# Shared expert of a decoder layer moved from the third stage into the last steps of the second stage's pipeline, and the padding rows with it

## The chip, the cores and the metric

The kernel runs on one core of a Trainium2 chip. The time is the device time of one execution in microseconds (us). The core has a matrix engine (TensorE, "PE" in the profile; its weight loads are "PEld"), a vector engine (VectorE, "DVE"), an activation engine (ScalarE, "ACT"), a general engine (GpSimd, "POOL") and a queue engine (SyncE, "SP"). Each engine works through its own list of instructions in order and waits on semaphores that others raise.

## The reference, cut to what matters

16 sequences of 128 tokens, 256 features. Three sublayers follow one another, each with a residual and a layer norm:

```
x = layernorm(x + self_attention(x))            # linear and windowed attention, gated
x = layernorm(x + cross_attention(x, context))  # 16 heads of 16
x = layernorm(x + mixed(x) + shared(x))
shared(x) = (silu(x @ Wsg.T) * (x @ Wsu.T)) @ Wsd.T     # 256 -> 256 -> 256
mixed(x)  = sum over the 4 experts picked of 32: weight * down_e(silu(gate_e(x)) * up_e(x))   # 256 -> 128 -> 256
```

The router's scores are sigmoid(x @ Wr.T) plus a bias; two of four groups are kept, then four experts of them.

## The kernel before, in words

The kernel has three stages with an all-engine barrier, a clearing of semaphores and another barrier between them. Stage 1 (`decoder_kernel`) is self attention. Stage 2 (`cross_attention`) is cross attention with its layer norm, the router, and the scatter of each token's row to the four experts' row lists in DRAM (`x_rows`). Stage 3 (`expert_layer`) is the shared expert, the routed experts and the last layer norm. Every fp32 product is made of three float16 products (high x high, high x low, low x high), so that each operand is split in two, mostly the high part by ACT (a copy to float16) and the low part by DVE or POOL (a subtraction).

**Stage 2** is a software pipeline over NB = 16 tiles of 128 tokens. Each engine has a loop over steps i, whose body is a hand written order of parts, and each part works on tile i minus its lag. PE's loop has 23 steps (`range(NB + 7)`), ACT's 23, DVE's 21 (`range(NB + 5)`), and POOL's 25. A PE step i answers to DVE step i - 2 and ACT step i + 1: a tile's scores are made in PE step n + 3, its minima in DVE step n + 1 and its exponentials in ACT step n + 4. The parts that the text names: `x2_T` (transposes of the normed tile, PE), `counts` (two matmuls over the picked experts, L1614), `logits` (L1606), `out_proj` (L1590, L1508), `transposed` and `weighted` (L1564, L1576), and on DVE `chosen` (MAX8 at L1425 to the mask `selc` at L1429), `places`, `scores_`, `st`, `x2`, `payload` (up to L1467). `chosen(i - 5)` is the first part of a DVE step. POOL's `scatter` (L1191) issues four indirect DMAs a tile, after `payload`.

PSUM has eight banks. One holds the attention output, and seven are shared by turns: `ORDERS` lists for each bank the uses in the order in which they take it within a step, `LAGS` the tile that each works on, and `Turns.wait` makes PE wait until the use before has been emptied.

The last steps have less in them. Attention scores end with PE step 18, `weighted` with step 19, `out_proj` with 20, `logits` with 21, `counts` with 22.

**Stage 3** begins with four things at once. SP loads a small table (`known`), waits for `fill_row` from DVE (the first row behind each expert's last), loads 32 row numbers into registers and issues 32 DMAs that write 128 padding rows each behind the 32 experts' lists (L1738); when these have landed it issues the gathers of the routed tiles (`xg`, L1755), 20 ahead. DVE makes the table of tiles in 19 chained steps and waits for one matmul of it on PE (L1956). PE, ACT and DVE run the shared expert in NCH = 8 chunks of 256 tokens (`shared_chunk`): 24 matmuls of 256 columns for gate and up, two banks each; Silu on ACT; the product on DVE; high part on ACT; low part on DVE; 12 matmuls of 256 columns for the down product; and DVE adds the result to `xs`. PE waits for all eight additions (`pe.wait_ge(sacc_r, NCH)`) before its first routed tile. Then 96 routed tiles run in a pipeline with lags of up to 10 steps, and after them the sum, the layer norm and the output.

Of the kernel before, what the change touches and what calls it, by code (L numbers as in the profile page):

```python
# [7 lines left out]
F16 = mybir.dt.float16  # L8
# [6 lines left out]
P = 128  # L15
# [15 lines left out]
PIECES = ((0, 1, 2), (3, 4))  # L31
ROUTE_SCALE = 2.5
# [47 lines left out]
def live(n, count=NB):  # L80
    return 0 <= n < count
# [7 lines left out]
class Turns:  # L89
    def __init__(self, orders, lags, reads, emptied):  # L90
        self.orders, self.lags, self.reads, self.emptied = orders, lags, reads, emptied

    def wait(self, pe, use, n):
        i = n + self.lags[use]
        for order in self.orders:
            k = order.index(use) if use in order else 0
            while use in order and i + k // len(order) >= 0:
# [3 lines left out]
                if 0 <= tile < NB:  # L101
                    pe.wait_ge(self.emptied[prev], self.reads.get(prev, 1) * (tile + 1))
                    break


def decoder_kernel(nc, x, ctx_t, wcat, vecs, rowvecs, rel_bias, consts, masks, experts, rbias_d, out):
# [3 lines left out]
    with es:  # L110
# [846 lines left out]
        c.scattered = [sem(f"scattered{k}") for k in range(RR)]  # L957
        kept = len(stage_sems)
# [29 lines left out]
def cross_attention(nc, c, ctx_t, experts, consts, rbias_d, out):  # L988
# [4 lines left out]
    with ExitStack() as st:  # L993
        def s2(name, shape, dt=F32):
# [5 lines left out]
        x1 = s2("x1", [P, 2, 2, D], F16)  # L1000
        x1T = s2("x1T", [P, 2, 2, KT, P], F16)
# [23 lines left out]
                "XT": 0, "P0": 3, "XPK": 2, "P2": 3, "XPQ": 1}  # L1025
# [4 lines left out]
                  ["S1", "XT"],  # L1030
                  ["XT2", "XWO", "XPQ"],
                  ["S0", "XPK"]]
# [5 lines left out]
        wait_turn = Turns(ORDERS, LAGS, {"XPK": 2}, emptied).wait  # L1038
# [68 lines left out]

        with nc.Block() as block:
            @block.sync
            def _(sp):  # L1110
# [23 lines left out]
                for i in range(NB + 7):  # L1134
# [3 lines left out]
                    context(i)  # L1138

# [68 lines left out]
            def _(act):  # L1208
# [90 lines left out]
                for i in range(NB + 7):  # L1299
                    ao_high(i - 6)  # L1300
                    pT_high(i - 5, 2)
                    xv_high(i - 4)
# [16 lines left out]
                    x1T_(i - 1)  # L1319
                    xq_high(i - 2)  # L1320

            @block.vector
            def _(dve):
# [145 lines left out]
                for i in range(NB + 5):  # L1469
# [25 lines left out]
            def _(pe):  # L1495
# [121 lines left out]
                for i in range(NB + 7):  # L1617
# [13 lines left out]
                    x1_T(i)  # L1631
                    transposed(i - 3, 0)
                    k_proj(i - 2)
                    transposed(i - 3, 2)
                    q_proj(i - 1)
                    weighted(i - 3, 0)


def expert_layer(nc, c, consts, out):
# [3 lines left out]
    CT = 2  # L1643
    NCH = NB // CT
    CW = CT * P
# [8 lines left out]
    with ExitStack() as st:  # L1654
# [19 lines left out]
        fill_row = s3("fill_row", [P, NE], U32)  # L1674

        with ExitStack() as before_tail:
# [5 lines left out]
            sgate = s3t("sgate", [P, 2, KT, CW])  # L1682
# [363 lines left out]
```

## Time and profile before

| | us |
|---|---|
| median of 3 runs (801.82 to 803.7) | 803.7 |
| the profiled execution's own time | 802.68 |
| its span in the profile | 800.9 |
| stage 1 to the barrier's exit at | 270.9 |
| stage 2, up to the barrier's exit at | 557.9 |
| shared expert, up to the last addition's end at | 599.2 |
| routed tiles, up to the last matmul near | 746 |
| sum, layer norm, output, up to | 800.9 |

Positions are counted from the start of the span. The own time is 1.8 us longer than the span, for what lies around it. The mean TensorE clock granted over the run is 0.866 of full speed.

### The profile page before, as it was taken

How to read it: one execution, taken by the hardware profiler on the slowest of the kernel's cores; microseconds unless marked ns; L12 is line 12 of the kernel's file. 1: busy time of each engine (PE TensorE's matmuls, PEld its weight loads, DVE VectorE, ACT ScalarE, POOL GpSimd, SP SyncE). 2: the span in 40 equal slices, each digit the busy share in tenths (PEclk: the TensorE clock that was granted, in tenths of full speed). 3: DMA queues.
4: the chain of work that ended last, by engine and by line, in shares of the span. 5: the costliest groups of instructions: out<-in, count | busy, mean ns of one | idle time of the engine just before them, and what ended most of it. 6: DMA issues, size and time to landing. Idle time of an engine off the chain costs nothing. (4 is left out here: it accounts for less than half of the span.)

```text
span 800.9 us, 24293 instructions
## 1 busy us (share of the span) xinstructions
PE 624.3 (78%) x7778; PEld 518.9 (65%) x7778; DVE 586.5 (73%) x2170; ACT 524.8 (66%) x1542; POOL 533.2 (67%) x689
## 2 busy tenths in 40 slices
PE   3899999999998488878777888631889999999100
PEld 2688888888888366756666666421679887777100
DVE  5898888888885367999999999882546655555495
ACT  5699999898887299878787787520228765555000
POOL 5877989999898535477767766663004765556684
PEclk9899999999999789787978787655899999999655
DMA  9200000000000122333543354241942555452383
GB/s 323 64 19 2 2 3 14 21 3 3 2 2 4 46 73 68 100 114 115 147 125 119 116 155 129 93 151 55 211 135 79 148 161 154 142 170 85 139 271 117
DMA packets 57131, 77.68 MB, mean 97 GB/s; under 512 B 8488, under 2 KB 46512, under 8 KB 56880
## 3 DMA queue, kind: packets, MB, share of 16 engines
q1 hardware_dynamic: 46208, 56.37, 24.7%
q0 software_dynamic: 7680, 16.87, 5.8%
q10 hardware_dynamic: 3120, 2.88, 1.1%
q8 instruction: 67, 1.10, 0.6%
q14 instruction: 56, 0.46, 0.2%
HBM read 44.39 MB, written 27.49 MB: 90 GB/s over the span
## 5 line engine op out<-in xcount | busy, mean ns | idle before, releaser
L1772 POOL DMA_INDIRECT y_rows<-yo,xg x96 | 94.7, 986 | 98.2 <-DVE yo L1886 60.0
L1886 DVE TENSOR_SCALAR yo<-bank,xg 128x256 f32<-128x256 f32 x96 | 46.4, 484 | 57.2 <-PE bank L1995 56.7
L1259 ACT ACTIVATE scx<-bank,mnx 128x128 f32<-128x128 f32 x256 | 73.9, 408 | 18.9 <-DVE mnx L1333 18.7
L1934 PE MATMUL bank<-gT,we_hi 128*128 128x128 f16 x768 | 79.1, 219 | 4.5 <-DVE eh L1896 3.6
L500 ACT ACTIVATE sc<-sc,mn 128x128 f32<-128x128 f32 x256 | 79.6, 396 | 0.0
L1191 POOL DMA_INDIRECT x_rows<-rows,slot_ix x64 | 63.5, 992 | 21.6 <-issue 18.3
L1162 POOL TENSOR_TENSOR we_lo<-east,we_hi 128x256 f16<-128x256 f32 (+1 forms) x80 | 59.3, 768 | 11.4 <-ACT we_hi L1233 11.1
L1934 PEld LDWEIGHTS bank<-gT,we_hi 128*128 (+1 forms) x768 | 51.8, 96 | 19.9 <-issue 9.9
L674 DVE CUSTOM_DVE_ANT_0 sc<-bank,rel 128x128 f32<-128x128 f32 x256 | 57.8, 286 | 8.7 <-PE bank L783 8.6
L1808 ACT ACTIVATE gT<-bank 128x512 f16<-128x512 f16 x96 | 56.4, 591 | 7.9 <-PE bank L1985 7.7
L1813 ACT ACTIVATE eh_hi<-eh 128x128 f16<-128x128 f32 x96 | 29.7, 309 | 46.8 <-DVE eh L1896 46.2
L1564 PE MATMUL bank<-ident,scx 128*128 128x128 f32 x256 | 51.5, 340 | 2.9 <-ACT scx L1259 2.8
L1934 PE MATMUL bank<-gT,we_lo 128*128 128x128 f16 x384 | 53.1, 218 | 0.0
L1339 DVE TENSOR_TENSOR pTx_lo<-bank,pTx_hi 128x512 f16<-128x512 f32 x64 | 43.6, 681 | 5.2 <-ACT pTx_hi L1267 4.8
L683 DVE TENSOR_TENSOR pT_lo<-bank,pT_hi 128x512 f16<-128x512 f32 x64 | 43.1, 681 | 5.0 <-ACT pT_hi L507 4.9
L830 PE MATMUL bank<-hT,w_hi 128*128 128x128 f16 x384 | 42.6, 227 | 3.3 <-DVE q_lo L655 2.3
L1333 DVE TENSOR_REDUCE mnx<-bank 128x4 f32<-128x512 f32 x64 | 42.5, 673 | 1.1 <-DVE rows L1458 0.3
L507 ACT ACTIVATE pT_hi<-bank 128x512 f16<-128x512 f32 x64 | 37.9, 592 | 6.8 <-PE bank L805 5.0
L1267 ACT ACTIVATE pTx_hi<-bank 128x512 f16<-128x512 f32 x64 | 40.0, 632 | 1.9 <-PE bank L1564 1.8
L793 PE MATMUL bank<-ident,sc 128*128 128x128 f32 x256 | 40.0, 279 | 0.4 <-ACT sc L500 0.4
L1564 PEld LDWEIGHTS bank<-ident,scx 128*128 128x128 f32 x256 | 35.4, 174 | 4.6 <-ACT scx L1259 4.6
L1985 PE MATMUL bank<-ident,xg 128*128 128x128 f16 x384 | 36.6, 218 | 1.6 <-DVE xs L1876 0.8
(291 smaller groups left out, 2441.6 us busy)
## 6 DMA issues: line engine op xcount, KB each, us to landing
xg<-x_rows SPq DMA_DIRECT2D x96, 129.0 KB, 2.6
east<-in_experts SPq DMA_DIRECT2D x32, 384.0 KB, 3.5
rows<-xhl SPq DMA_DIRECT2D x16, 512.0 KB, 4.5
yg<-y_rows SPq DMA_DIRECT2D x16, 512.0 KB, 4.5
x_rows<-padrow SPq DMA_DIRECT2D x33, 129.0 KB, 4.1
wst<-in_wcat SPq DMA_DIRECT2D x8, 256.0 KB, 5.6
cst<-in_ctx_t SPq DMA_DIRECT2D x16, 128.0 KB, 3.3
out<-fin ACTq DMA_DIRECT2D x16, 128.0 KB, 3.1
```

The source lines that it names most:

```text
L500: done = act.activation(sc[:, g, j], sc[:, g, j], ACT.Exp, bias=mn[:, n % 2, g, j:j + 1], scale=-1.0)
L674: dve.tensor_tensor_reduce(out=sc[:, g, j], in0=sc_bank[g][:, j * P:(j + 1) * P], in1=rel[:, g, j], scale=-1.0, scalar=-NEG, op0=ALU.add, ...
L683: dve.tensor_tensor(pT_lo[:, g % 2], pT_bank[g][:].rearrange("p (h k) -> p h k", h=GH), pT_hi[:, g % 2], ALU.subtract).then_inc(pT_rd[g], 1)
L1162: pool.tensor_tensor(pair(shared.we_lo, piece, n), arrived(piece), pair(shared.we_hi, piece, n), ALU.subtract).then_inc(we_lo_done[k], 1)
L1191: pool.indirect_dma_start(shared.x_rows, bass.IndirectOffsetOnAxis(ap=slot_ix[:, n, k:k + 1], axis=0), rows4[:, q, k], None).then_inc(shar ...
L1259: done = act.activation(scx[:, g, j], sc_bank[g][:, j * P:(j + 1) * P], ACT.Exp, bias=mnx[:, n % 2, g, j:j + 1], scale=-1.0)
L1339: dve.tensor_tensor(pTx_lo[:, g % 2], pT_bank[g][:].rearrange("p (h k) -> p h k", h=GH), pTx_hi[:, g % 2], ALU.subtract).then_inc(xpT_rd[g ...
L1564: last = pe.transpose(pT_bank[g][:, j * P:(j + 1) * P], scx[:, g, j], ident[:])
L1772: pool.indirect_dma_start(c.y_rows, bass.IndirectOffsetOnAxis(ap=xg_word(U32, n % G, 0), axis=0), yo[:, n % YO], None, bounds_check=NDEST ...
L1808: act.activation(gT[:, n % U], GT_BANK[n % len(GT_BANK)], ACT.Copy).then_inc(gt_r, 1)
L1886: dve.tensor_scalar(yo[:, n % YO], DN_BANK[n % 2][:, 0:D], xg_word(F32, n % G, 1), None, ALU.mult).then_inc(yo_r, 1)
L1934: done = pe.matmul(o[:, m * width:(m + 1) * width], lhs(x_, k, m), rhs(y_, k, m), start=t == 0, stop=t == 5)
```

## The change

In stage 3 the shared expert and the padding rows are gone, with their buffers and semaphores. PE's first routed tile no longer waits for additions; the table's matmul is put in front of step 5 of the routed loop (`i == L_GU + 1`), in the bank of the odd down products, so the down product of tile 1 waits for the table.

In stage 2 the shared expert becomes three more uses of the shared banks: `GU0`, `GU1` (gate and up of one of the chunk's two tiles, in one bank) and `SD` (the down product). `FIRST_SH` = 17: chunk n has its gate and up products in PE step n + 17 (24 matmuls of 128 columns for each tile), its Silu in ACT step n + 18, its products and low part in DVE step n + 16, its high part in ACT step n + 19, its down product in PE step n + 18 and its addition in DVE step n + 17. The hidden tile has one buffer instead of two. The loops grow: PE to 26 steps, ACT to 27, DVE to 25. ACT's Silu and Exp now alternate: chunks 0 to 4 follow the exponentials of attention or of the router in ACT steps 18 to 22.

The row numbers of the padding are made by DVE in its step 20. SP writes half of the padding rows after its loop in stage 2, ACT the other half after its own loop. The first gathers of stage 3 wait for both.

```diff
+NCH = NB // 2
+FIRST_SH = 17
...
         LAGS = {...
-                "XT": 0, "P0": 3, "XPK": 2, "P2": 3, "XPQ": 1}
+                "XT": 0, "P0": 3, "XPK": 2, "P2": 3, "XPQ": 1, "GU0": FIRST_SH, "GU1": FIRST_SH, "SD": FIRST_SH + 1}
...
-                  ["S1", "XT"],
-                  ["XT2", "XWO", "XPQ"],
-                  ["S0", "XPK"]]
+                  ["S1", "XT", "GU0"],
+                  ["XT2", "XWO", "XPQ", "GU1"],
+                  ["S0", "XPK", "SD"]]
...
+        def pad_rows(eng, kind, part):
+            eng.wait_ge(shared.fill_r, 1)
+            _, rows = nc.values_load_multi_w_load_instructions(
+                shared.fill_row[0:1, part * NE // 2:(part + 1) * NE // 2], engines=[kind], min_val=0, max_val=NE * CAP - P,
...
+            for v in rows:
+                eng.dma_start(shared.x_rows[bass.ds(v, P), :], shared.padrow[:]).then_inc(shared.filled, 16)
...
+                pad_rows(sp, mybir.EngineType.SP, 0)
...
+                def sh_gate(n, b):
+                    if live(n, NCH):
+                        act.wait_ge(filled[f"GU{b}"], n + 1)
+                        wait(act, shlo_r, n)
+                        act.activation(shid[:, b], gate_up(b, 0), ACT.Silu).then_inc(emptied[f"GU{b}"], 1)
+
+                def sh_high(n):
+                    if live(n, NCH):
+                        act.wait_ge(emptied["GU0"], 2 * (n + 1))
+                        act.wait_ge(emptied["GU1"], 2 * (n + 1))
+                        wait(act, filled["SD"], n)
+                        act.activation(sh_hi[:], shid[:], ACT.Copy).then_inc(shhi_r, 1)
...
+                for i in range(NB + 11):
                     ao_high(i - 6)
                     pT_high(i - 5, 2)
+                    sh_high(i - FIRST_SH - 2)
...
                     x1T_(i - 1)
+                    sh_gate(i - FIRST_SH - 1, 0)
                     xq_high(i - 2)
+                    sh_gate(i - FIRST_SH - 1, 1)
+                pad_rows(act, mybir.EngineType.Activation, 1)
...
+                def sh_mult(n, b):
+                    if live(n, NCH):
+                        dve.wait_ge(emptied[f"GU{b}"], 2 * n + 1)
+                        dve.tensor_tensor(shid[:, b], gate_up(b, 1), shid[:, b], ALU.mult).then_inc(emptied[f"GU{b}"], 1)
+
+                def sh_low(n):
+                    if live(n, NCH):
+                        dve.wait_ge(shhi_r, n + 1)
+                        wait(dve, filled["SD"], n)
+                        dve.tensor_tensor(sh_lo[:], shid[:], sh_hi[:], ALU.subtract).then_inc(shlo_r, 1)
+
+                def sh_add(n):
+                    if live(n, NCH):
+                        dve.wait_ge(filled["SD"], n + 1)
+                        dve.tensor_tensor(xs[:, 2 * n:2 * n + 2], room["SD"][:].rearrange("p (b d) -> p b d", b=2), xs[:, 2 * n:2 * n + 2], ALU.add
+                                          ).then_inc(emptied["SD"], 1)
...
+                for i in range(NB + 9):
                     chosen(i - 5)
+                    sh_mult(i - FIRST_SH + 1, 0)
                     xq_low(i)
                     p_low(i - 2, 2)
+                    sh_mult(i - FIRST_SH + 1, 1)
                     xv_low(i - 1)
+                    sh_add(i - FIRST_SH)
                     mins(i - 1, 1)
                     weights(i - 5)
                     places(i - 5)
+                    if i == NB + 4:
+                        dve.tensor_scalar(shared.fill_row[:], shared.count[:], -1.0, None, ALU.add).then_inc(shared.fill_r, 1)
                     mins(i - 1, 0)
+                    sh_low(i - FIRST_SH + 1)
                     scores_(i - 4)
...
+                for i in range(NB + 10):
                     x2_T(i - 6)
...
                     transposed(i - 3, 1)
                     x1_T(i)
+                    sh_in(i - FIRST_SH, 0)
                     transposed(i - 3, 0)
                     k_proj(i - 2)
+                    sh_out(i - FIRST_SH - 1)
                     transposed(i - 3, 2)
                     q_proj(i - 1)
+                    sh_in(i - FIRST_SH, 1)
                     weighted(i - 3, 0)
...
-                sp.wait_ge(filled, 16 * NE)
+                sp.wait_ge(c.filled, 16 * NE)
...
-                unrolled(1, shared_chunk, NCH)
-                pe.wait_ge(sacc_r, NCH)
-
-                owners = [e * EI for e in range(NE)]
-
-                def tile(i, s, h):
+                owners = [e * EI for e in range(NE)]
+
+                def tile(i, s, h):
+                    if i == L_GU + 1:
                         pe.wait_ge(tab_step, TAB_STEPS)
                         pe.matmul(TAB_BANK[:, 0:2 * P], c.ones[:], diag[:].rearrange("p s t -> p (s t)"), start=True, stop=True).then_inc(tab_ps, 1)
```

## Rows read from the trace of the kernel before

**Rows 1.** The chain that ended last, stage 3: start us, length us, what.

```profile
566.43 1.22 PE bank L1956 x2
567.65 25.77 PE bank L1934 x228
593.45 0.61 ACT sgate L1796
594.82 0.70 DVE shid L1867
595.54 0.64 ACT sh_hi L1799
596.20 0.70 DVE sh_lo L1871
...
598.47 0.70 DVE xs L1876
...
601.67 0.67 PE bank L1934 x12
```

**Rows 2.** Busy time by stretch, stage 3: length, each engine's busy time, clock, DMA.

```profile
557.90:562.60 4.70, 4.62 (x23) 3.34 (x24) 1.47 (x5) 1.88 (x2) 0.12 (x1) 0.51 0.38 119
...
570.00:598.00 28.00, 27.08 (x249) 24.00 (x247) 14.13 (x22) 8.45 (x14) 0.00 (x0) 1.00 0.73 173
```

**Rows 3.** Timeline of SP, stage 3: start us, length us, queue, line, DMAs issued.

```profile
559.71 17.96 SPq L1738 DMA_DIRECT2D x_rows<-padrow  x32
582.55 9.37 SPq L1755 DMA_DIRECT2D xg<-x_rows  x20
```

**Rows 4.** Timeline around the barrier behind stage 2, POOL and ACT.

```profile
550.15 0.96 POOL L1191 DMA_INDIRECT x_rows<-rows,slot_ix  x1 [0.30 <-issue]
557.94 0.12 POOL L1768 MEMSET cums<- 128x32 f32 x1 [6.83 <-POOLq L963]
557.94 1.28 ACT L1796 ACT_TABLE_LOAD   x1 [21.33 <-PEq L963]
...
560.74 0.60 ACT L1796 ACTIVATE sgate<-bank 128x512 f32<-128x512 f32 x1 [1.51 <-PE bank L1934]
```

**Rows 5.** Timeline around the barrier behind stage 1, DVE and ACT.

```profile
268.80 0.41 DVE L734 TENSOR_SCALAR xs<-yt,mv,rstd 128x256 f32<-128x256 f32 x1 [0.75 <-POOL rstd L326]
270.96 0.31 ACT L1209 ACTIVATE ident<-ident 128x128 f16<-128x128 f32 x1 [6.43 <-PEq L946]
```

**Rows 6.** Busy time by stretch, DVE steps 16 to 19 of stage 2 (columns as in Rows 2).

```profile
498.21:513.14 14.93, 9.59 (x118) 7.24 (x112) 14.00 (x48) 10.82 (x31) 10.31 (x14) 0.71 0.31 99
513.14:523.92 10.78, 6.56 (x66) 5.15 (x66) 8.90 (x42) 2.94 (x7) 7.09 (x11) 0.66 0.28 81
523.92:534.08 10.16, 4.10 (x22) 2.79 (x22) 7.81 (x36) 2.63 (x6) 7.19 (x10) 0.50 0.47 164
534.08:541.04 6.96, 1.19 (x10) 1.11 (x10) 5.71 (x34) 0.20 (x1) 3.99 (x5) 0.50 0.42 147
```

**Rows 7.** Timeline of PE, last steps of stage 2, and its first rows of stage 3.

```profile
522.63 0.58 PE L1516 MATMUL bank<-ident,xhl 128*128 128x128 f16 x4 [2.88 <-POOL xhl L1182]
...
532.83 0.59 PE L1516 MATMUL bank<-ident,xhl 128*128 128x128 f16 x4 [4.32 <-POOL xhl L1182]
...
557.98 1.01 PE L1934 MATMUL bank<-hT,w_hi 128*128 128x256 f16 x4 [14.84 <-PEq L963]
```

**Rows 8.** Timeline of DVE, step 18 of stage 2.

```profile
528.60 0.43 DVE L1379 BATCH_NORM_STATS2 xstats<-bank 128x6 f32<-128x256 f32 x1 [1.11 <-PE bank L1508]
```

**Rows 9.** Timeline of ACT, step 21 of stage 2.

```profile
526.22 0.20 ACT L1297 ACTIVATE rt_e<-bank 128x32 f32<-128x32 f32 x1 [1.70 <-PE bank L1606]
```

**Rows 10.** The padding rows' line on SP: duration ns min/median/max, first and last start.

```profile
L1738 SPq DMA_DIRECT2D x_rows<-padrow x32: 332/332/371, 559.7 to 577.3; - x32
...
DMA to landing us min/median/max: 2.1/4.1/5.1
```

**Rows 11.** The output's line on ACT's queue (columns as in Rows 10).

```profile
L1824 ACTq DMA_DIRECT2D out<-fin x16: 338/338/455, 766.2 to 793.2; - x16
```

More of the change, by code:

```diff
@@ L1037, in cross_attention, with gate_up @@
         emptied = {u: x2_ready if u == "XWO" else sem(f"xrd_{u}") for u in LAGS}
[L1038 removed]
+        wait_turn = Turns(ORDERS, LAGS, {"XPK": 2, "GU0": 2, "GU1": 2}, emptied, {"GU0": NCH, "GU1": NCH, "SD": NCH}).wait
+        shhi_r, shlo_r = sem("shhi_r"), sem("shlo_r")
+        def gate_up(b, j):
+            return room[f"GU{b}"][:, j * D:(j + 1) * D].rearrange("p (k t) -> p k t", k=KT)
         def flipped(u):
@@ L1106, in arrived @@
             return east[:, k, at:at + 2 * EI * (1 + piece // 4)].rearrange("p (h w) -> p h w", w=2 * EI)
+        def pad_rows(eng, kind, part):
+            eng.wait_ge(shared.fill_r, 1)
+            _, rows = nc.values_load_multi_w_load_instructions(
+                shared.fill_row[0:1, part * NE // 2:(part + 1) * NE // 2], engines=[kind], min_val=0, max_val=NE * CAP - P,
+                skip_runtime_bounds_check_because="an expert's rows start at a multiple of CAP and are at most CAP - P")
+            for v in rows:
+                eng.dma_start(shared.x_rows[bass.ds(v, P), :], shared.padrow[:]).then_inc(shared.filled, 16)
         with nc.Block() as block:
@@ L1615, in counts, with sh_in, sh_out @@
                         pe.matmul(room["CN"][:, NE:2 * NE], shared.ones[:], selc[:, n % 2], start=True, stop=True).then_inc(filled["CN"], 1)
-                for i in range(NB + 7):
+                def sh_in(n, b):
+                    if live(n, NCH):
+                        wait_turn(pe, f"GU{b}", n)
+                        for j, col in enumerate((C_SG, C_SU)):
+                            for m in range(KT):
+                                t = 0
+                                for x_, y_ in ((0, 0), (1, 0), (0, 1)):
+                                    for k in range(KT):
+                                        done = pe.matmul(gate_up(b, j)[:, m], W[x_][:, k, col + m * P:col + (m + 1) * P], shared.xT[:, 2 * n + b, y_, k],
+                                                         start=t == 0, stop=t == 5)
+                                        t += 1
+                        done.then_inc(filled[f"GU{b}"], 1)
+                def sh_out(n):
+                    if live(n, NCH):
+                        H = (sh_hi, sh_lo)
+                        wait_turn(pe, "SD", n)
+                        pe.wait_ge(shlo_r, n + 1)
+                        products("SD", lambda s, k, m: H[s][:, m, k], lambda s, k, m: W[s][:, k, C_SD:C_SD + D], 2, D)
+                for i in range(NB + 10):
                     x2_T(i - 6)
@@ L1730, in _ @@
                 sp.dma_start(known[:], consts[:, 2 * P + NE:2 * P + 2 * NE + 1]).then_inc(k_in, 16)
-                sp.wait_ge(fill_r, 1)
-                for half_ in range(2):
-                    _, rows = nc.values_load_multi_w_load_instructions(
-                        fill_row[0:1, half_ * NE // 2:(half_ + 1) * NE // 2], engines=[mybir.EngineType.SP], min_val=0, max_val=NE * CAP - P,
-                        skip_runtime_bounds_check_because="an expert's rows start at a multiple of CAP and are at most CAP - P")
-                    for v in rows:
-                        sp.dma_start(c.x_rows[bass.ds(v, P), :], c.padrow[:]).then_inc(filled, 16)
                 for q in range(RR):
```

77 lines of the change are left out of this document (13 added, 64 removed).

## The prediction

> **What bounds the kernel now.** I read the chain that ended last first, to see what stage 3 waits for. Its opening is the shared expert on PE alone: the table's matmul, 228 matmuls in 25.77 us, one last pass through ACT and DVE, and the addition that ends at 599.17; routed tiles start there, and the second gate and up group, routed step 5, starts at 601.67 [rows 1]. The busy times by stretch say the same: from 570 to 598 PE is busy 27.08 of 28.00 us at a granted clock of 1.00, the 2.4 GHz level, DVE for half of it [rows 2]. The padding rows are written meanwhile (SP issues them up to 577.7, gathers start at 582.55) and are not on the path, since PE is still 16 us from needing a tile [rows 3].
>
> Then I read the end of stage 2 by DVE's steps. Step 16, the last with attention scores, takes 14.93 us with DVE busy 14.00. Steps 17, 18 and 19 take 10.78, 10.16 and 6.96, with PE busy 6.56, 4.10 and 1.19 and ACT 2.94, 2.63 and 0.20 [rows 6]. So PE and ACT have room there, but DVE, a row of short dependent operations, hardly has. Step 20 starts where step 19 ends, at 541.04; call that moment T. Its payload feeds POOL's last scatter, which ends at 551.11, and stage 3 starts only 6.8 us behind it [rows 4]. Behind stage 1, where POOL issued no indirect DMA, the same two barriers took 1.75 us from DVE's last end (269.21) to the first instruction [rows 5]. I read the other 5.1 us as POOL's, for finishing its indirect DMAs.
>
> **What stage 3 gives back.** All of the shared expert leaves, but not all of its 41 us is won: the table chain stays. Its matmul can start 8.5 us into the stage (566.43 - 557.94) and takes 1.2 [rows 1, 4]. That stage start is S. In the old kernel step 5's gate and up group ran at 601.67, in the new one at S + 9.7. Routed tiles also start cold: the first 4.70 us of PE in this stage, after 15 us of idleness, had a clock of 0.51, the 1.2 GHz level, against 1.00 later [rows 2, 7]. Half speed for some 4 us costs 2 us, so the point compared is S + 11.7. The change breaks even when S = 601.67 - 11.7 = 590.0, that is when stage 2 ends 32.0 us later than before. The rest of the sum is how much of these 32.0 us the moved work uses.
>
> **What stage 2 has to take.** Per chunk, by the last chunk of before: 0.70 product, 0.70 low part and 0.70 addition on DVE, here the product in two halves of about 0.41, as a 128x256 operation took [rows 5]; 0.6 (two of 0.4) Silu and 0.64 high part on ACT; 36 matmuls of 256 columns on PE, 25.77 / 228 = 0.113 us each, so 4.1 us at 2.4 GHz, and 8.1 at 1.2 GHz [rows 1]. (The 48 of 128 columns are the same columns; the weights are loaded twice as often. At 0.113 a pair I cost that at nothing, since the k products of stage 2 overlap their loads; uncovered it is under 1 us a chunk and inside the clock's range.) So DVE gets 2.2 us per step, PE 4.1 to 8.1, ACT 1.4 and its table loads.
>
> *Steps 16 to 19.* PE's part of chunk 0 stands ahead of the k products, transposes and scores of the last tile, which DVE's minima need; with DVE's own 1.5 us that makes step 16 some 3 us longer. In step 17 PE has again 4 to 8 us more between transposes that DVE waits for, against idle gaps of a few us: 3. In steps 18 and 19 DVE has 2.2 us more, of which a wait of up to 1.1 us for the output product swallows a part [rows 8]; PE's added work lies in gaps of 2.9 and 4.3 us before the transposes of the next tile [rows 7] and overruns them by 0 to 4: 2 each. Sum 10, with 5 (DVE's additions alone, less gaps) and 15 (PE at 1.2 GHz in all four) as ends. New T: 551.
>
> *From T to the last high part.* Chunk 4's low part is done about 4.7 us after T (mask 1.0, two products 0.8, addition 0.7, weights and places 1.5, low 0.7). Chunks 5, 6 and 7 now run with one hidden buffer: down product and second gate and up group on PE (two thirds of a chunk, 2.7 or 5.4), Silu 0.4, product 0.4, high 0.64, low 0.70, and only then the next. This is 4.9 us a chunk at 2.4 GHz and 7.5 at 1.2. The last high part ends at T + 4.7 + 3 x 2.7 + 2 x 2.2 + 1.5 = T + 18.7, or T + 26.8 at the low clock. PE would be busy some 80% in it, which in the rows goes with clocks between the levels; I take T + 22. Before, this place was held by POOL's end, 10.1 us after T [rows 4, 6]. So +11.9. POOL's own path, with its 6.8 us, now ends at T + 17 and is covered; without the cover it would cost what it did before.
>
> *Padding rows.* SP's 16 are issued from about T + 4 on, 0.56 us each (17.96 / 32) [rows 3], done by T + 14, hidden by the chunks. ACT's 16 stand behind its last high part, and nothing hides them: loading 16 row numbers about 1.3 us (SP's first issue, at 559.71, came 1.8 us into stage 3 with the wait for DVE's row numbers in it [rows 3]), then 16 issues. An issue on ACT's queue lasts 338 ns, on SP's 332 [rows 10, 11], so I take SP's pace, 0.50 to 0.56. Sum +10. Low bound 7 (338 ns and nothing between), high 12. Behind them the landing (median 4.1 us [rows 10]) is covered by the barrier and the table chain: last gather possible near S + 2.5, first tile in by S + 6.5, table only at S + 8.5.
>
> *Barrier.* 1.75 in place of 6.8 us, because ACT, not POOL, is last: -5.1 [rows 4, 5]. The opposite bound is 0, if the 6.8 us belong to the stage and not to POOL.
>
> *ACT's tables.* Silu needs a load: 1.28 us, at the head of stage 3 [rows 4]. Exp and Silu alternating over ACT steps 18 to 22 make nine loads, 11.5 us, one of stage 3 gone. The load of stage 3 started at once, and its Silu 1.5 us behind the load's end, on PE's matmuls [rows 4], and ACT idles 1.7 us before the router's exponential [rows 9], so I cost them at 0 while that idle time lasts.
>
> **Sum.** 10 + 11.9 + 10 - 5.1 = 26.8 us used of 32.0: 5.2 us won. The profiled execution's 802.68 becomes 797.5. The median of the runs is 1.0 us above it, so the median comes to 798.5; I put the prediction at 798.
>
> **Rivals.**
> 1. *PE stays at 1.2 GHz through the tail* (slower). PE's clock was 0.50 to 0.71 in these steps [rows 6]. Each chunk then costs 8.1 us in front of the transposes: T at +15, last high part at T + 26.8: used 15 + 16.7 + 10 - 5.1 = 36.6, loss 4.6, 807. It decides from 5.2 us more than I took, which is about two thirds of the way from my middle to that end. Against it: continuous matmuls brought the clock to 1.00 in stage 3 [rows 2].
> 2. *Table loads are dearer than their row.* Between the load's end and the Silu lay 1.5 us (559.22 to 560.74) in which PE's wait could hide more of it [rows 4], so a switch may cost up to 2.8 us. Beyond the idle 1.7 us that is 1.1 for each of the four Exp loads on the router's loop: +4.4, no change, 802. The Trainium skill, ScalarE: Activation LUTs, "What ACT_TABLE_LOAD costs", says that every switch to another set takes 1283 ns and a drain of about 1380 ns, and asks to do all of one set's functions before the other's. By that rule this rival holds. The row agrees with 1283 ns and can't show the drain.
> 3. *The 6.8 us are the stage's.* 5.1 us less gain: 802.6, no change. For it: that the row names POOL's queue proves no cause. Against: 1.75 us at the other barrier.
> 4. *The tail takes it all* (better case). DVE's additions alone (+5), clock at 2.4 GHz (T + 18.7), ACT issues in 8.5: used 5 + 8.6 + 8.5 - 5.1 = 17, won 15, 788.
>
> **How the numbers follow.** My forecast, with its own range of 792 to 801, gets 0.57; rival 1 0.14, rival 2 0.07, rival 3 0.07, rival 4 0.15. About 0.3%, 2.4 us, is what a measurement of this kernel can tell from no change. Faster: 0.57 + 0.15 + a little of rivals 2 and 3 that lie under it, 0.74; within: 0.13; slower: 0.13. The range of 8 in 10 reaches from 789 to 806 and leaves out the outer parts of rivals 4 and 1.
>
> **What the profile after would show.** If I am right: the barrier's exit near 585 (before 557.94); ACT's last instructions ahead of it are 16 issues over 8 to 9 us while PE and DVE idle; POOL done at least 10 us before the exit; DVE's `selc` of the last tile near 552; a chunk every 5 to 7 us in the last three; the second gate and up group some 10 us after the exit; routed tiles unchanged at their pace. Wrong would be: an exit set by DVE or POOL; steps 17 to 19 longer by more than 4 us each; ACT gaps of over 1.3 us ahead of `rt_e` that no wait explains; a first routed tile that waits for a gather and not for the table.

## The result, and the profile after

The changed kernel takes 795.6 us (median of four runs, 790.91 to 796.45) against 802.88 for the kernel before on the same chip (four runs, 801.82 to 803.70). The ratio is 0.9896, with a 95% interval of 0.986 to 0.9932. The forecast was 798, with a range of 789 to 806. The profiled execution of the changed kernel is the fastest of its runs, 790.91 us, so the trace shows more gain than the median: its span is 11.8 us shorter (789.1 against 800.9), the median 7.3.

First the busy times by stretch after the change, with columns as in [rows 2]. The first four stretches are DVE's steps 16 to 19 and answer to [rows 6]. The fifth and sixth run from T (the start of step 20) to the last addition, the seventh up to the exit from the barrier, the eighth to the second gate and up group.

```profile
496.39:515.69 19.30, 16.58 (x174) 13.51 (x174) 15.57 (x51) 13.90 (x37) 10.31 (x13) 0.65 0.24 76
515.69:529.07 13.38, 9.94 (x99) 8.81 (x100) 10.77 (x45) 7.68 (x15) 8.04 (x10) 0.62 0.23 65
529.07:541.28 12.21, 8.58 (x116) 7.34 (x113) 9.56 (x40) 7.02 (x13) 8.14 (x11) 1.00 0.40 137
541.28:550.30 9.02, 6.05 (x67) 5.55 (x68) 7.54 (x38) 4.26 (x6) 3.96 (x5) 0.81 0.35 119
550.30:556.31 6.01, 3.69 (x49) 3.26 (x47) 5.46 (x24) 1.40 (x3) 3.72 (x4) 1.00 0.25 88
556.31:572.95 16.64, 11.20 (x157) 10.09 (x155) 7.11 (x13) 3.81 (x8) 4.16 (x4) 1.00 0.76 183
572.95:580.40 7.45, 0.00 (x0) 0.00 (x0) 0.00 (x1) 0.00 (x0) 0.00 (x1) 0.70 1.02 213
580.40:589.90 9.50, 4.45 (x37) 3.96 (x38) 4.65 (x20) 2.75 (x6) 0.12 (x1) 0.52 0.64 169
```

The lengths of the four steps are to be set beside those of [rows 6]: +4.4, +2.6, +2.05 and +2.06 us, 11.1 in all. In steps 17 to 19 PE now has 9.94, 8.58 and 6.05 us of work where it had 6.56, 4.10 and 1.19, and the granted clock is 0.62, 1.00 and 0.81 where it was 0.66, 0.50 and 0.50. The moved work went with a higher clock in steps 18 and 19, and not in steps 16 and 17 (0.65 and 0.62 where it was 0.71 and 0.66).

The chain that ended last, from the sixth chunk of the shared expert to routed step 5, answers to [rows 1].

```profile
560.21 1.47 PE bank L1568 x12
561.68 1.35 PE bank L1685 x24
563.05 0.39 ACT shid L1323
563.47 0.43 DVE shid L1509
563.98 0.64 ACT sh_hi L1330
564.64 0.70 DVE sh_lo L1515
565.48 1.47 PE bank L1568 x12
...
569.25 0.63 ACT sh_hi L1330
569.88 0.61 ACTq L1121
570.66 0.38 ACTq L1125
...
578.28 4.89 DMA x_rows<-padrow
583.26 2.15 DMA xg<-x_rows
585.46 2.05 PE bank L1996 x16
587.51 1.28 PE bank L1964 x12
588.79 0.43 PE bank L1996 x4
589.21 0.71 PE bank L1974 x2
589.93 0.67 PE bank L1964 x12
```

Four things are to be seen. A chunk is a ring through three engines: down product of one chunk and the rest of the next chunk's gate and up group on PE (L1568, L1685), Silu on ACT, product on DVE, high part on ACT, low part on DVE, and only then the next down product, 5.27 us later (560.21 to 565.48). Behind the last high part, at 569.88, ACT's queue issues its 16 padding blocks until 578.62. The barrier's exit, 580.40, is not in the chain at all: the chain goes through the landing of the last padding block (4.89 us), since the gathers wait for it. And the table's matmul (L1974) runs behind the first routed tiles, not ahead of them. The barrier itself is read from the timelines of POOL, ACT and SP, which answer to [rows 3, 4]:

```profile
561.20 0.96 POOL L1211 DMA_INDIRECT x_rows<-rows,slot_ix  x1 [0.30 <-issue]
...
570.66 7.96 ACTq L1125 DMA_DIRECT2D x_rows<-padrow  x16
...
580.40 0.12 POOL L1831 MEMSET cums<- 128x32 f32 x1 [18.24 <-POOLq L966]
```

```profile
555.60 9.01 SPq L1125 DMA_DIRECT2D x_rows<-padrow  x16
```

SP's 16 blocks are issued by 564.61, under the chunks. POOL's last scatter ends at 562.16 and its next instruction is 18.24 us behind it, so POOL no longer holds the barrier. ACT does: 1.8 us from its last issue's end to the exit, where POOL's end had 6.8 us behind it before [rows 4].

### The profile page after: what moved, and what is told of

It reads as the page before. It is cut to its first block, busy times and chain, and to the rows that moved or that the text cites. A ratio compares the mean times of both kernels' runs of the same rounds, so it can differ in the third digit from the quotient of the medians.

```text
span 789.1 us, 24713 instructions
## 1 busy us (share of the span) xinstructions
PE 619.5 (78%) x7970; PEld 521.1 (66%) x7970; DVE 586.9 (74%) x2178; ACT 535.8 (68%) x1558; POOL 535.1 (68%) x689
## 4 chain that ended last, share of the span: by engine, by line
DVE 25%; PE 25%; issue 7%; ACT 3%; DMA 2%; POOL 1%; ACTq 1%; DVEq 0%; SPq 0%; POOLq 0%
PE bank L1964 10%; PE bank L2008 4%; DVE pTx_lo L1376 4%; PE bank L1996 4%; DVE mnx L1370 3%; PE bank L1568 2%; PE bank L1624 1%; DVE yquad L1935 1%; DVE fstats L1941 1%; DVE ysum L1938 1%; ACT scx L1279 1%; PE bank L1685 1%; DVE xk_lo L1384 1%; ACTq L1125 1%; DVE wpick L1501 1%
## 5 line engine op out<-in xcount | busy, mean ns | idle before, releaser
L1182 POOL TENSOR_TENSOR we_lo<-east,we_hi 128x256 f16<-128x256 f32 (+1 forms) x80 | 60.0, 776 | 11.4 <-ACT we_hi L1253 11.1
L1996 PE MATMUL bank<-ident,xg 128*128 128x128 f16 x384 | 37.7, 223 | 13.2 <-DMA xg<-x_rows 13.2
L1636 PE MATMUL bank<-xv_hi,pTx_hi 128*128 128x17 f16 x256 | 26.4, 175 | 16.6 <-DVE pTx_lo L1376 16.6
```

The source lines that it names most:

```text
L1182: pool.tensor_tensor(pair(shared.we_lo, piece, n), arrived(piece), pair(shared.we_hi, piece, n), ALU.subtract).then_inc(we_lo_done[k], 1)
L1996: done = pe.transpose(GT_BANK[n % len(GT_BANK)][:, part, k], xg[:].bitcast(F16)[:, n % G, (part * KT + k) * P:(part * KT + k + 1) * P], c. ...
```

## The experiments

In what follows T is the start of DVE step 20, as in the prediction, S the exit from the barrier behind stage 2. Each kernel was timed beside the kernel before on the same chip, and the ratios are to that.

**The change again, as a base for the others.** No edit.

> The changed kernel once more, unaltered, beside the others of this set. Both theories: 795.6 us median within its own spread of 791 to 796.5. It is there because its runs spread by 5.5 us, so that the other kernels of the set are read against it.

Measured: 792.36 us (six runs, 788.66 to 794.36) against 801.55, ratio 0.9888 (0.9863 to 0.9913). T at 551.73, last high part at T + 19.6, exit at T + 30.1, the first gather's issue at T + 32.1. These are the same distances as in the first trace, but for the gather (there T + 33.0). So the gain is 7 to 9 us, and the profile at hand, 11.8 us, is on the lucky side of it: its step 16 began 1.8 us earlier than in the kernel before, here 0.6 us earlier.

**All padding rows on SP.** The second half leaves ACT's queue, whose 16 issues stood behind its last high part.

```diff
                 pad_rows(sp, mybir.EngineType.SP, 0)
+                pad_rows(sp, mybir.EngineType.SP, 1)
...
-                pad_rows(act, mybir.EngineType.Activation, 1)
```

> All 32 padding writes of stage 2 are issued by SP, none by ACT. Theory A (ACT's 16 issues behind its last high part are on the path, nothing hides them): SP starts near 555.6 and issues at 0.50 to 0.56 us each, so it ends at 571.6 to 573.6, beside the last addition at 572.95; the barrier's exit comes near 575 in place of 580.4 and the time falls by 5 us, to about 790.5. Rival B (the exit is set by the landing of the padding rows or by POOL's indirect DMAs, not by an issue): the exit stays near 580 and the time within 1 us of the changed kernel.

Measured: 789.83 us (787.12 to 790.05), ratio 0.9842 (0.9821 to 0.9864), 2.5 us under the change. The timeline of SP:

```profile
558.68 19.08 SPq L1125 DMA_DIRECT2D x_rows<-padrow  x32
...
582.11 8.02 SPq L1818 DMA_DIRECT2D xg<-x_rows  x15
```

32 issues in 19.08 us are 0.60 each, with SP's second load of row numbers (L1121, 1.29 us) among them, and the exit follows 1.76 us behind SP's end at 577.76, T + 26.1 in place of T + 30.1. So ACT's issues did lie on the path, as term "Padding rows" had it, but all of them together are not 8.7 us of gain when gone: SP's own end takes half of it back. Theory A's direction was right and its 5 us too large, since it had SP at 0.50 to 0.56. That the median fell by 2.5 and not by 4 us may be the start of the tail: in this profile step 15, in code that the edit does not touch, took 17.2 us where it took 15.5 in the changed kernel.

**The shared expert moved, the padding rows left in stage 3.**

```diff
-                pad_rows(sp, mybir.EngineType.SP, 0)
-                pad_rows(act, mybir.EngineType.Activation, 1)
...  (stage 3, SP, ahead of the gathers)
+                sp.wait_ge(c.fill_r, 1)
+                for half_ in range(2):
+                    _, rows = nc.values_load_multi_w_load_instructions(...)
+                    for v in rows:
+                        sp.dma_start(c.x_rows[bass.ds(v, P), :], c.padrow[:]).then_inc(c.filled, 16)
```

> The shared expert stays in stage 2, but SP writes the 32 padding blocks at the head of stage 3, as before. Theory A (the two moves need each other): the exit comes at 572.95 + 1.8 = 574.8, but the first gather follows the padding rows and comes 24.6 us later as before (582.55 - 557.94), at 599.4, and the routed tiles start some 16 us later than in the changed kernel: about 811 us, slower than the kernel before. Rival B (the padding rows stay hidden, behind the table's chain and first tiles): the 5.6 us of an earlier exit are won, 790.

Measured: 809.67 us (808.33 to 811.24), ratio 1.0109 (1.0087 to 1.0132). Theory A had 811. The exit came earlier, T + 24.3, and that was of no use. SP's timeline, and PE's first routed instruction:

```profile
577.39 18.31 SPq L1807 DMA_DIRECT2D x_rows<-padrow  x32
599.15 6.98 SPq L1824 DMA_DIRECT2D xg<-x_rows  x13
```

```profile
601.25 2.02 PE L2002 MATMUL bank<-ident,xg 128*128 128x128 f16 x13 [27.99 <-DMA xg<-x_rows]
```

In the kernel before, PE was in the middle of the shared expert when these rows were written [rows 1, 3]. With the shared expert gone they are on the path: PE stands for 28.0 us ahead of its first routed tile, where it stands for 13.2 in the changed kernel.

**The padding rows moved, the shared expert left in stage 3.** This is the kernel before with the two calls of `pad_rows` at the ends of SP's and ACT's stage 2, the row numbers computed by DVE in its step 20, and the loop in stage 3 taken out.

```diff
+                pad_rows(sp, mybir.EngineType.SP, 0)
...
+                pad_rows(act, mybir.EngineType.Activation, 1)
...
+                    if i == NB + 4:
+                        dve.tensor_scalar(shared.fill_row[:], shared.count[:], -1.0, None, ALU.add).then_inc(shared.fill_r, 1)
...  (stage 3, SP)
-                sp.wait_ge(fill_r, 1)
-                for half_ in range(2):
...
-                        sp.dma_start(c.x_rows[bass.ds(v, P), :], c.padrow[:]).then_inc(filled, 16)
```

> The kernel before with only the padding rows moved to the end of stage 2, half on SP and half on ACT; the shared expert stays in stage 3. Theory A (they were hidden behind PE's shared expert, and in stage 2 they are hidden behind POOL's 6.8 us): 802.9 us, no change, exit near 558. Rival B (they cost something where they were, by the DMA engines that they fill beside the shared expert, or ACT's 10 us of loading and issuing delay the exit): a difference of over 2.4 us one way or the other.

Measured: 810.68 us (808.41 to 811.11), ratio 1.0117 (1.0095 to 1.0139), 9.1 us slower than before, where theory A had expected no difference. Timelines of SP, of ACT's queue and of POOL:

```profile
544.24 13.05 SPq L1115 DMA_DIRECT2D x_rows<-padrow  x16
```

```profile
544.32 13.35 ACTq L1115 DMA_DIRECT2D x_rows<-padrow  x16
```

```profile
562.12 0.12 POOL L1771 MEMSET cums<- 128x32 f32 x1 [12.31 <-POOLq L964]
```

Two queues issue at once and each issue takes 0.82 us, 0.41 us a block together, where SP alone took 0.56 with a load of row numbers among them [rows 3] and ACT alone 0.50 in the chain above. The DMA engines are full meanwhile (share 1.07 to 1.14 from 545 to 560, where the kernel before had 0.29 to 0.04). ACT's last issue ends at 557.67, the exit follows 4.4 us later and not 1.8, and it is 12.3 us behind POOL's last scatter where before it was 6.8. T was 1.3 us earlier in this profile (539.72), so from T to the exit it is 22.4 us against 16.9. In the profile this makes the table's matmul 5.9 us late (572.33 against 566.43), of which 4.2 are the exit and 1.7 the load of `known`, which takes 5.04 us to land where it took 3.3. The span is 5.7 us longer. The profiled run is the fastest of its four, and where the other 3 us of the median lie, no trace shows.

Together these two runs say that neither half of the change gains alone: +8.1 and +9.1 us apart, 9.2 us gained when joined.

**No table loads.** Silu becomes Tanh in the shared expert, so the output of that expert is another. Tanh is in the table that Exp uses in this kernel: of the nine loads at L1317 and L1323 none is left, and one comes back in stage 3 for the routed experts.

```diff
-                        act.activation(shid[:, b], gate_up(b, 0), ACT.Silu).then_inc(emptied[f"GU{b}"], 1)
+                        act.activation(shid[:, b], gate_up(b, 0), ACT.Tanh).then_inc(emptied[f"GU{b}"], 1)
```

> The changed kernel with Tanh in place of Silu in the shared expert (another function of the same cost, so the output is not the reference's): stage 1 uses Exp and Tanh with no table load between them, so the nine loads of stage 2 go and one at the head of stage 3 comes. Theory A (the loads lie in ACT's waits for PE and for the router): within 1 us of the changed kernel, that is 791.5 to 792.5 in this set's terms. Rival B (a switch costs up to 2.8 us and the four Exp loads delay the router's loop by 1.1 us each): 4.4 us faster, 788.

Measured: 793.49 us (six runs, 791.82 to 794.23), ratio 0.9887 (0.9857 to 0.9916). The ratio of the change itself was 0.9888. Steps 16 to 19 took 19.1, 13.5, 12.2 and 9.0 us, as with the loads (19.3, 13.4, 12.2 and 9.0). 11.5 us of table loads on ACT are worth nothing measurable here. These are the groups by line of the changed kernel with their loads (idle time before them last):

```profile
L1323 ACT ACT_TABLE_LOAD x5 | 6.4, 1283 | 0.7 <-DVE sh_lo L1515 0.6
L1317 ACT ACT_TABLE_LOAD x4 | 5.1, 1283 | 0.1
```

and one of them in ACT's timeline:

```profile
512.98 1.15 ACT L1279 ACTIVATE scx<-bank,mnx 128x128 f32<-128x128 f32 x4
514.15 1.28 ACT L1323 ACT_TABLE_LOAD   x1
515.44 0.66 ACT L1323 ACTIVATE shid<-bank 128x256 f32<-128x256 f32 x2
```

The load starts 20 ns behind the exponentials (512.98 + 1.15 = 514.13) and the Silu 10 ns behind the load.

**The shared expert left out.** It is computed nowhere, so the output lacks it.

```diff
-NCH = NB // 2
+NCH = 0
```

> The changed kernel with the shared expert left out everywhere (no chunks), the padding rows where the change puts them; the output lacks the shared expert. It prices the shared expert in the tail. Theory A: step 20 starts near 541 as in the kernel before, the exit comes near 562 as in the kernel with only the padding rows moved, and the routed tiles' step 5 comes 9.5 us behind it, at 571.5: 18.5 us earlier than in the changed kernel, about 774. So the shared expert costs some 18 us in the tail, where it cost over 40 in stage 3. Rival B (its work is nearly hidden and the growth of stage 2 comes from the padding rows): over 785.

Measured: 776.17 us (774.91 to 777.39), ratio 0.967 (0.9633 to 0.9708). T is 541.02, that of before (541.04), and the exit T + 23.6. SP's and ACT's 16 issues take 12.86 and 12.78 us, and the exit is 6.2 us behind ACT's last and 13.5 behind POOL's last scatter. This kernel is 26.1 us faster than before (802.24 on its chip), not 41: the exit is 6.7 us later than before (564.59 against 557.94), with the padding writes beside POOL's last scatters, and the table's matmul comes 10.4 us behind it (574.97), 8.5 before [rows 1, 4]. The shared expert in its new place then costs 26.1 less the 9.2 us that the change won over the kernel before on its own chip, about 17 us.

**The shared expert one step earlier.**

```diff
-FIRST_SH = 17
+FIRST_SH = 16
```

> FIRST_SH = 16: each chunk one step earlier, so that one chunk less (5.3 us of chain) is left behind the router's last step, and one more lies in a step with full attention work. Theory A (a chunk in a full step costs as much as step 16 grew, 4.4 us): 5.3 less and 4.4 to 5 more, no change to speak of, 791 to 793. Rival B (step 16 grew for other reasons, a start of the matmuls at the low clock, and a second full step takes the work for DVE's 2.2 us): 3 us faster, 789.

Measured: 801.69 us (ten runs, 800.12 to 806.22), ratio 1.0002 (0.998 to 1.0024). Both theories missed: they had 791 to 793 and 789, and it was 9 us slower than the change. DVE's steps 14, 15 and 16 took 17.5, 23.8 and 25.1 us, in the changed kernel 14.8, 15.5 and 19.3. PE's timeline has two waits:

```profile
484.58 0.28 PE L1685 MATMUL bank<-hT,w_hi 128*128 128x128 f16 x2 [4.76 <-DVE xq_lo L1390]
```

```profile
506.12 0.61 PE L1568 MATMUL bank<-w_hi,sh_hi 128*128 128x256 f16 x2 [3.59 <-DVE xk_lo L1384]
```

The second half of a chunk's gate and up group (GU1) shares a bank with the q projection (XPQ), the down product (SD) with the k projection (XPK). One step earlier the last q projection has just been written to that bank and is read by DVE only in its turn; PE waits for it, the work queued behind it on PE (the transposes of the exponentials) comes late, and DVE waits 5.54 us for the part of `pTx_hi` that comes out of them. T moved from 550.30 to 565.99, and 4.3 us came back behind it (exit T + 25.8, one chunk fewer there). Step 17 is the first in which that bank has no q projection. This one kernel points at the banks and not at PE's room in [rows 6] as what fixes the place of the work; the same start with other banks was not tried.

**The down product at the end of PE's step.** Gate and up of the next chunk go to PE whole, ahead of the down product, which waits for the hidden parts.

```diff
-                    sh_out(i - FIRST_SH - 1)
                     transposed(i - 3, 2)
                     q_proj(i - 1)
                     sh_in(i - FIRST_SH, 1)
+                    sh_out(i - FIRST_SH - 1)
                     weighted(i - 3, 0)
```

> In PE's loop the down product of the chunk before is put behind both gate and up groups instead of between them. Theory A (the 5.27 us from chunk to chunk behind the router are a chain down product, second gate and up group, Silu, product, high, low): the second group now runs while ACT and DVE make the high and low parts, and a chunk takes PE's 4.2 us; three chunks, about 3 us faster, 789.5. Rival B (PE's order doesn't bind there): no change.

Measured: 789.75 us (788.23 to 790.65), ratio 0.9841 (0.9803 to 0.988). The chain that ended last:

```profile
559.74 2.85 PE bank L1685 x48
562.60 1.31 PE bank L1568 x12
563.91 2.68 PE bank L1685 x48
```

That is 12.5 us under the kernel before, where the change won 9.2. PE now has no gap. A chunk takes 4.0 us, which is PE's own time, in place of 5.27; ACT's and DVE's parts lie under it. The last high part ends at T + 15.4 instead of T + 19.6, the exit is at T + 25.9 instead of T + 30.1.

**24 blocks on SP and 8 on ACT, with the down product last.** Both queues should end at about the same time.

```diff
-        def pad_rows(eng, kind, part):
+        def pad_rows(eng, kind, lo, hi):
...
-                pad_rows(sp, mybir.EngineType.SP, 0)
+                pad_rows(sp, mybir.EngineType.SP, 0, 16)
+                pad_rows(sp, mybir.EngineType.SP, 16, 24)
...
-                pad_rows(act, mybir.EngineType.Activation, 1)
+                pad_rows(act, mybir.EngineType.Activation, 24, 32)
```

> Both gains together: the down product last in PE's step, 24 padding blocks on SP and 8 on ACT. With T the start of DVE's step 20: ACT's last high part ended at T + 15.4 with that order; SP's 24 issues end near T + 19, ACT's 8 near T + 20.5, the last addition at T + 19.2, so the exit comes near T + 22.3, against T + 30.1 in the changed kernel and T + 26 in each of the two single edits. Theory A (what ends last sets the exit, and the table's chain follows at a fixed 9.3 us): about 3.6 us better than either, 786. Rival B (the DMA engines are the floor: 32 blocks at 0.6 us from T + 5.3, and the gathers wait for their landing): exit earlier, but the routed tiles start no earlier than with all blocks on SP, 789.5.

Measured: 788.73 us (788.19 to 789.24), ratio 0.9826 (0.9804 to 0.9849). The exit came at T + 22.7, 3.3 us earlier than in the run before, and the gathers only at T + 28.3. The chain that ended last says why:

```profile
573.01 7.92 DMA x_rows<-padrow
```

The last padding block takes 7.92 us to land where it took 4.89 in the changed kernel. Rival B had it. The end of the issues moved, the end of the writing did not.

**All on SP, with the down product last.** The second half of the padding on SP, as above, and the down product last, as above:

```diff
+                pad_rows(sp, mybir.EngineType.SP, 1)
...
-                pad_rows(act, mybir.EngineType.Activation, 1)
...
-                    sh_out(i - FIRST_SH - 1)
...
+                    sh_out(i - FIRST_SH - 1)
```

> All padding blocks on SP, and the down product last. Theory A: SP's 32 issues, 19 us from T + 5.3, are what ends last, so the earlier end of the chunks is hidden behind them: exit at T + 26 as with all blocks on SP alone, 789.8, although each edit alone gave 2.5 us. Rival B (the chunks' chain still decides): the gains add, 787.

Measured: 788.04 us (787.36 to 789.16), ratio 0.982 (0.9792 to 0.9848). The timeline of SP:

```profile
556.31 19.18 SPq L1125 DMA_DIRECT2D x_rows<-padrow  x32
...
579.91 10.49 SPq L1818 DMA_DIRECT2D xg<-x_rows  x20
```

The first issue comes at T + 5.3, 32 blocks take 19.2 us, 0.60 each on average, and the gathers start at T + 28.9. The chain that ended last shows what the average hides:

```profile
565.56 1.31 SPq L1121
567.04 0.33 SPq L1125
567.55 0.33 SPq L1125
```

SP issues a block every 0.51 to 0.52 us, and stands once for 1.31 us to load the second 16 row numbers (L1121). In four kernels, this one and the three others with a shorter tail (all on SP, down product last, 24 and 8), the table's matmul starts at T + 34.4 to T + 34.6, whatever their exit (T + 22.7 to T + 26.2). Their medians, 788.0 to 789.8 us, can't be told apart (the intervals of the four ratios overlap), so the times do not decide between rival B's 787 and theory A's 789.8. The exit does: it came at T + 26.2, as theory A had it.

**Half of the padding rows in stage 2, on SP alone, the shared expert in stage 3.** The kernel with only the padding rows moved, and ACT's half put back at the head of SP's stage 3.

```diff
-                pad_rows(act, mybir.EngineType.Activation, 1)
...  (stage 3, SP)
+                _, rows = nc.values_load_multi_w_load_instructions(c.fill_row[0:1, NE // 2:NE], ...)
+                for v in rows:
+                    sp.dma_start(c.x_rows[bass.ds(v, P), :], c.padrow[:]).then_inc(c.filled, 16)
```

> The kernel before with 16 padding blocks issued by SP at the end of stage 2 and 16 by SP at the head of stage 3; the shared expert stays in stage 3. It asks why moving them all there, half on each queue, cost 9 us. Theory A (issued from two queues at once they fill the 16 DMA engines, share 1.07 to 1.14 from 545 to 560, while POOL's last indirect DMAs are to be finished and the next stage's table is to be fetched): one queue for half the time leaves the exit near 558 and the time at 802 to 803. Rival B (any padding write there delays POOL's end): exit and time at least 3 us later.

Measured: 806.05 us (ten runs, 804.13 to 808.53) against 801.82, ratio 1.0045 (1.0028 to 1.0062). T is 541.87, 0.8 us later than before. The timelines of SP and POOL:

```profile
546.37 8.33 SPq L1115 DMA_DIRECT2D x_rows<-padrow  x16
```

```profile
562.15 0.12 POOL L1776 MEMSET cums<- 128x32 f32 x1 [10.20 <-POOLq L964]
```

POOL's last scatter ends at 551.95. SP has issued its 16 by 554.70, and ACT has none; even so the exit is 10.2 us behind that scatter, where it was 6.8, and 7.5 us behind SP. It is 4.2 us later than before, and so is the median. Rival B had this, theory A missed. The distance from POOL's last scatter to the exit is longer when padding writes go beside the scatters. It is not the landing of these writes that the exit waits for: in the changed kernel the last block lands at 583.17, 2.8 us behind the exit. The nearest explanation, that POOL's own indirect DMAs finish later when other writes share the DMA engines (share 1.09 from 550 to 555, where before it was 0.15), is not shown.

## Why the prediction was right

The mechanism held step by step, and most terms were a little too large. In the order of the prediction, from the profiled execution:

*Steps 16 to 19* (+10): the four steps grew by 11.1 us. Step 16 began 1.8 us earlier than in the kernel before, so T moved by 9.3 (550.30 against 541.04). Step 16 was under-sized: it took 4.4 more, not 3. What made the term small was the early start of step 16, not the steps (in the change run again T is 551.73, 10.7 later). What the prediction had not named is a wait for a bank: the last tile's scores wait for the bank that chunk 0's gate group holds until DVE's product has read it. PE's timeline:

```profile
497.91 0.40 PE L1614 MATMUL bank<-xk_hi,xq_hi 32*128 32x256 f16 x2 [2.24 <-DVE shid L1509]
```

The kernel with the shared expert one step earlier shows what this sharing costs when the work is put where the banks are busier. Steps 17 to 19 were foreseen with 3, 2 and 2, and took 2.6, 2.1 and 2.1.

*From T to the last high part* (+11.9): T + 19.6, not T + 22, so +9.5. The ring was the right picture (4.9 us a chunk at 2.4 GHz foreseen, 5.27 measured), and the clock was the over-sized term: it stood at 1.00, the 2.4 GHz level, from T to the end of the chunks. The reason given for T + 22, a busy share that goes with clocks between the levels, did not hold: from 556.31 to 572.95 PE was busy 11.20 of 16.64 us and the clock was 1.00. The down product at the end of PE's step showed the ring from the other side: with the hidden parts under PE's work a chunk costs 4.0.

*Padding rows* (+10): 8.7, from 569.88 to 578.62, at 0.50 us a block. Taking them off ACT's queue gave 2.5 us of the median, and shortened T to the exit by 4.0. It could not give 8.7, because SP's 32 issues, with the second load of row numbers among them, end only at T + 24.4.

*Barrier* (-5.1): 1.8 us behind ACT, so -5.05. In the four kernels with a shorter tail, too, the exit comes 1.76 to 1.78 us behind the last issue. Rival 3, that the 6.8 us belong to the stage, fell in the changed kernel. But those 6.8 us are not a fixed price of POOL's either: with padding writes beside its last scatters they were 10.2 to 13.5 us (the shared expert left out, or in stage 3). With no chunks at all the term fails: there the exit is 6.2 us behind ACT's last issue. With 24 and 8 blocks, an exit 11.1 us behind POOL's last scatter, it still held.

*Sum*: 9.3 + 9.5 + 8.7 - 5.05 = 22.5 us used, against 26.8. The point of comparison, routed step 5, came 9.5 us behind the exit (9.7 foreseen), and the 2 us set aside for a cold clock were not spent. Busy times by stretch, the changed kernel:

```profile
585.40:589.93 4.53, 4.47 (x37) 3.99 (x38) 2.63 (x15) 2.78 (x6) 0.00 (x0) 0.54 0.92 260
589.93:593.93 4.00, 4.00 (x75) 4.00 (x73) 2.13 (x9) 3.16 (x11) 0.00 (x0) 1.00 0.86 236
```

The clock is at the 1.2 GHz level for 4.5 us of PE's work, and these lie ahead of step 5, where the table chain would have made PE wait anyway; from 589.93 on it is 1.00. From step 5 to the end the two kernels take the same time, 199.17 and 199.23 us. So 4.3 (terms) + 0.2 + 2.0 = 6.5 us more than the 5.2 foreseen, 11.7 of the 11.8 by which the span is shorter. The medians differ by 7.3, 9.2 when the change was run again; 2.6 to 4.5 us of what this trace shows are the luck of its run. The same luck flatters the forecast: its sum, 797.5 for the profiled execution, was 6.6 us above the 790.91 measured, while 798 for the median was only 2.4 above, because the profiled run lies 4.7 us under its median, where the sum had allowed 1.0. By the change run again the gain was 9.2 us where 4.9 was forecast.

*The point that was wrong on its own terms* is the last tile's cover: "first tile in by S + 6.5, table only at S + 8.5". Both times held (S + 5.0 and S + 8.1), but PE's own work on the first tiles between them was left out, and the sign that it named as wrong, a first routed tile that waits for a gather and not for the table, is what came. The padding block lands 4.89 us behind its issue, the gathers' first issue is at S + 2.9, the first transposes at S + 5.1, and PE, at the low clock, works on the first routed tiles until S + 8.6. DVE's `diag`, which the table's matmul needs, is ready at 588.48, S + 8.1:

```profile
588.19 0.29 DVE L1905 TENSOR_SCALAR diag<-ident,block 128x128 f32<-128x128 f32 x1
```

So PE's chain behind the gather decided by half a microsecond, and not the table. It cost nothing to speak of here, but it is what limits each better version: in the kernel with 24 and 8 blocks the exit came 3.3 us earlier than with 16 and 16 (down product last in both), and the gathers 0.1 us (T + 28.3 against T + 28.4).

*Rival 1* (low clock, slower) fell: 1.00 where the chunks are the path. Its turning point was put too far out: 5.2 us of the 9.8 between the middle (26.8) and that end (36.6) is about half of the way, not two thirds. *Rival 2* (table loads dearer than their row) fell by the run without loads: 0.9887 beside 0.9888. The Trainium skill, ScalarE: Activation LUTs, "What ACT_TABLE_LOAD costs", speaks of a drain of about 1380 ns with every switch; the 1283 ns of the load agree with the rows, a drain does not show between rows that are 10 and 20 ns apart. *Rival 4* (the tail takes it all, 788) was half right: the clock, and ACT's 8.5 us of issues, came true, DVE's +5 did not. 788.0 is what the best version reached, by another way.

**What stays open.** Which event ends POOL's wait at the stage's end: the kernels show that it lengthens with padding writes beside the scatters, and not what it waits for. There is no kernel in which the padding is not written near POOL's last scatters and yet in stage 2. The floor of T + 34.5 that four kernels share is read from their traces. The writing rate of 32 blocks of 129 KB is its likely cause: from 565 to 573 the DMA engines have a share of 0.96 to 1.15 in all four and move 225 to 237 GB/s. But only with 24 and 8 blocks did earlier issues lead to a longer landing; in the other three the last issue itself ends at T + 24.1 to T + 24.5 and lands 4.5 to 4.7 us behind its start. Fewer or smaller padding blocks were not tried, so the cause is not shown. The 3 us of median by which the kernel with only the padding moved is slower than its profile shows have no cause either.

## What to carry to other kernels

Two moves that are each a loss can be a gain together, when one is the cover of the other: the shared expert hid the padding in stage 3, so moving it alone left PE waiting for 28 us, 15 more than in the changed kernel, and moving the padding alone made the barrier 4 us later. Ask of a block of work that is moved what it was hiding. When work is put into a pipeline's last steps, read which bank or buffer it shares and with whose last use, before reading which engine has room; and order it so that the engine that is the bound (here PE) has its next block queued ahead of the one that waits. When an earlier end of the issues makes the last landing longer by as much, the rate of the transfers is the limit and not who issues them.

## What the hardware showed that I had not expected

- Two queues that issued at once shared one rate (the kernel with only the padding rows moved). The issue itself, 332 to 338 ns alone, took 590 and 624 ns in the median (up to 1.09 us), 0.82 us from one to the next on each queue, and a block landed after 3.0 to 9.8 us (median 8.2) where it was 2.1 to 5.1 [rows 10]. The Trainium skill, DMA: Bandwidth & Descriptors, "Issuing engines are not separate DMA queues", says that DMAs run on the same 16 engines whoever issues them; the runs agree (0.41 us a block from two queues together, 0.50 to 0.52 from one).
- The distance from POOL's last indirect DMA to the barrier's exit was 6.8 us with a DMA share of 0.05 beside it, 10.2 with 16 plain blocks on one queue beside it, 12.3 and 13.5 with 32 on two.
- PE's clock was higher where more work was put between its old matmuls (0.50 to 1.00 in step 18, 0.50 to 0.81 in step 19), though not in steps 16 and 17. In 18 and 19 the added matmuls made part of their own room.
- A table load of 1.28 us on an engine with that much idle time, nine times, was worth nothing measurable.
